# Routing to the best two experts by two rounds of maxima instead of by pairs, and the gate bias added by VectorE instead of TensorE

## The chip, the cores and the metric

The kernel runs on one core of a Trainium2 chip. The metric is the device time of one execution in microseconds (us), the median over several. Three executions of the kernel before took 4944.28, 4973.12 and 4980.82 us; the profiled one, which is another, took 4966.12 us.

## The reference, cut to what matters

The program is a decoder of four layers over 16 sequences (batches) of 100 tokens with 128 features. Every layer has a self attention, a cross attention over a context of 1444 rows, and a feed forward; each adds its result to `x`. The feed forwards of layers 0, 1 and 3 are mixtures of experts with 8, 16 and 8 experts, of which each token uses its best two. For layer 3:

```python
logits = xf @ wg.T + bg
vals, idx = jax.lax.top_k(logits, TOP_K)          # TOP_K = 2
masked = jnp.full_like(logits, -jnp.inf)
masked = masked.at[rows, idx].set(vals)
weights = jax.nn.softmax(masked, axis=-1)
for e in range(NUM_EXPERTS):
    g = xf @ Wgate[e].T
    u = xf @ Wup[e].T
    h = g * jax.nn.sigmoid(g) * u
    out = out + h @ Wdown[e].T * weights[:, e:e + 1]
```

Layer 0 is of the same kind. In layer 1 there is no gate bias in the logits: the experts are picked by the logits plus a bias of their own (`expert_bias`), while the weights are the sigmoids of the logits without it, divided by their sum. When two logits are equal, `top_k` takes the one with the lower index first, and both versions of the kernel keep that.

## The kernel before, in words

One program runs through the stages of the reference in order. Each engine has its own instruction stream, written out by hand, and the order between engines is kept by semaphores alone; there is no planner. `x`, its normalised copy `xn`, and most working tiles lie in SBUF with 128 features on the partitions and the 1600 tokens along the columns. A large tile, `arena`, is shared by the stages. All small weights of a stage are packed in one tile (`w_const` for constants, `w_ff0`, `w_ff1`, `w_ff3` for the gates of the feed forwards; the profile cuts the number off), and each is loaded at the start of the program.

A routed feed forward (the function `feed_forward` of each engine's stream, with `route` for VectorE) runs like this.

1. After the layer normalisation TensorE computes the gate logits, one product for each of the 16 batches, with the tokens of the batch as the stationary operand: a 100 x E block of PSUM bank 0 for each batch (L3516). Where the stage has a gate bias (the first and the third), a product of a row of ones and the bias goes ahead of each of them into the same block (L3515). The last one raises `logits_ready`.
2. VectorE routes (L2436 to L2506). It copies the logits to SBUF (L2442), and in the stages with 8 experts subtracts each token's maximum (L2452, L2455). It then raises `weights_asked`, on which ScalarE computes the exponentials (L1782). Meanwhile VectorE compares every logit of a token with every other one, in tiles of 16 batches x E x E columns: equal to it and of lower index (L2463, L2466), greater than it (L2469), the sum of both (L2472), and a reduction to the rank (L2475). Experts of a rank under 2 are kept (L2478). Then it waits for the exponentials, masks them with that, sums, takes the reciprocal and multiplies (L2490 to L2503).
3. `weights_ready` releases TensorE, which transposes the weights batch by batch (L3521). ScalarE copies them to SBUF (L1787). SP stores them to DRAM (L952), waits for that, and only then loads the first expert's weights (L925) and the rows of its gate weights, spread over the partitions (L935).
4. POOL splits `xn` into a rounded part and a rest at the start of the stage in the stages with 8 experts (L1265, tiles `x_hi` and `x_lo`), later also each expert's weights and the gated tokens. TensorE, ScalarE and VectorE then work through the experts, 128 hidden features and 400 tokens at a time.

On VectorE each instruction of the route raises a semaphore at its end, on which the stream waits before the next one.

Long stages lie in between: the multi-head cross attention of layer 0 from 100 to 1480 us, and the narrow cross attention of layer 2, with 8 features a head, from about 2580 to 3460 us.

Of the kernel before, what the change touches and what calls it, by code (L numbers as in the profile page):

```python
# [23 lines left out]
ALU = mybir.AluOpType  # L24
# [257 lines left out]
def feed_parts(n, p):  # L282

    def wide(w):
        return w.transpose(1, 0, 2).reshape(w.shape[1], -1)

    if n == 0:
        return (chunks_of(wide(p["L0_ffn_w1"]), wide(p["L0_ffn_w3"]), p["L0_ffn_w2"].reshape(-1, 128)),
                dict(gate=p["L0_ffn_gate_w"], gate_b=p["L0_ffn_gate_b"][None]))
    if n == 1:  # L290
        up = [np.concatenate([wide(p[f"L1_ffn_w{k}"].transpose(0, 2, 1)), p[f"L1_ffn_sw{k}"].T], 1) for k in (1, 3)]
        down = np.concatenate([p["L1_ffn_w2"].transpose(0, 2, 1).reshape(-1, 128), p["L1_ffn_sw2"].T], 0)
        bias = [np.concatenate([p[f"L1_ffn_b{k}"].reshape(-1), p[f"L1_ffn_sb{k}"]]) for k in (1, 3)]
        return (chunks_of(up[0], up[1], down, *bias),
                dict(gate=p["L1_ffn_gate_w"].T, expert_b=np.tile(p["L1_ffn_expert_bias"], (128, 1)),
                     b2=p["L1_ffn_b2"], sb2=p["L1_ffn_sb2"][None]))
    if n == 2:
        return (chunks_of(p["L2_ffn_w1"][0], None, p["L2_ffn_w2"][0], p["L2_ffn_b1"][0]),
                dict(b2=p["L2_ffn_b2"][0][None], ln_g=column(p["L2_ffn_gamma"]), ln_b=column(p["L2_ffn_beta"])))
    if n == "g":  # L300
        return (chunks_of(p["L3_xattn_W1"], None, p["L3_xattn_W2"], p["L3_xattn_b1"]), dict(b2=p["L3_xattn_b2"][None]))
    return (chunks_of(wide(p["L3_ffn_Wgate"].transpose(0, 2, 1)), wide(p["L3_ffn_Wup"].transpose(0, 2, 1)),
                      p["L3_ffn_Wdown"].transpose(0, 2, 1).reshape(-1, 128)),
            dict(gate=p["L3_ffn_wg"].T, gate_b=p["L3_ffn_bg"][None]))


def film_parts(p):
# [70 lines left out]
def constants():  # L378

    i = np.arange(128)  # L380
    ident = np.eye(128, dtype=np.float32)
    mean = np.full((128, 128), 1 / 128, np.float32)
    ones = np.ones((128, 128), np.float32)
    row96 = np.zeros((C + 1, C + 1), np.float32)
    row96[C] = 1
    own_head = np.zeros((C + HEADS, HEADS), np.float32)
    for h in range(HEADS):
        own_head[C + h, h] = -1
    head_rows = (i[:, None] // 8 == i[None, :] // 8).astype(np.float32)

    def head_rows_of(n):

        at = np.arange(4 * n)
        return (i[:, None] == (at // n * 32 + at % n)[None, :]).astype(np.float32)

    return dict(ident=ident, mean=mean, ones=ones, row96=row96,
                head_cols=(i[:, None] // 8 % 4 == np.arange(4)[None, :]).astype(np.float32),
                rows8=head_rows_of(9), rows16=head_rows_of(17),
                own_head=own_head, head_rows=head_rows,
                zeros=np.zeros((HEADS, 128), np.float32),  # L400
                ones_row=np.ones((1, GT), np.float32),
                before=np.tile((np.arange(16)[None, :] < np.arange(16)[:, None]).astype(np.float32).reshape(1, -1), (128, 1)))


def build(nc, dram, where, out):
# [1413 lines left out]
    def _(dve):  # L1819
# [615 lines left out]
        def route(n):  # L2435

            cfg = FEED[FF[n]]
            E = cfg["E"]
            dve.wait_ge(s.logits_ready, 1)
            dve.sem_inc(s.logits_ready, -1)  # L2440
            lg, bi, rk, wt = (t[:, :, 0:E] for t in (logits, biased, rank, weight))
            nc.vector.tensor_copy(lg, ps[0:S, 0, 0:B * E].rearrange("p (b e) -> p b e", e=E)).then_inc(s.dve_done, 1)  # L2442
            dve.wait_ge(s.dve_done, 1)
            dve.sem_inc(s.dve_done, -1)
            by = lg
            if cfg.get("sigmoid"):
                nc.vector.tensor_tensor(bi, lg, W(FF[n], "expert_b")[0:S, :].unsqueeze(1).to_broadcast([S, B, E]), ALU.add).then_inc(s.dve_done, 1)
                dve.wait_ge(s.dve_done, 1)
                dve.sem_inc(s.dve_done, -1)
                by = bi  # L2450
            else:
                nc.vector.tensor_reduce(best[:, :], lg, AX.X, ALU.max).then_inc(s.dve_done, 1)  # L2452
                dve.wait_ge(s.dve_done, 1)
                dve.sem_inc(s.dve_done, -1)
                nc.vector.tensor_tensor(lg, lg, best[:, :].unsqueeze(2).to_broadcast([S, B, E]), ALU.subtract).then_inc(s.dve_done, 1)  # L2455
                dve.wait_ge(s.dve_done, 1)
                dve.sem_inc(s.dve_done, -1)
            dve.sem_inc(s.weights_asked, 1)
            p1 = pairs[:, 0:B * E * E].rearrange("p (b e f) -> p b e f", e=E, f=E)
            p2 = pairs2[:, 0:B * E * E].rearrange("p (b e f) -> p b e f", e=E, f=E)  # L2460
            mine, other = by.unsqueeze(3).to_broadcast([S, B, E, E]), by.unsqueeze(2).to_broadcast([S, B, E, E])
            before = W("const", "before")[0:S, :].rearrange("p (e f) -> p e f", f=16)[:, 0:E, 0:E]
            nc.vector.tensor_tensor(p1, other, mine, ALU.is_equal).then_inc(s.dve_done, 1)  # L2463
            dve.wait_ge(s.dve_done, 1)
            dve.sem_inc(s.dve_done, -1)
            nc.vector.tensor_tensor(p1, p1, before.unsqueeze(1).to_broadcast([S, B, E, E]), ALU.mult).then_inc(s.dve_done, 1)  # L2466
            dve.wait_ge(s.dve_done, 1)
            dve.sem_inc(s.dve_done, -1)
            nc.vector.tensor_tensor(p2, other, mine, ALU.is_gt).then_inc(s.dve_done, 1)  # L2469
            dve.wait_ge(s.dve_done, 1)  # L2470
            dve.sem_inc(s.dve_done, -1)
            nc.vector.tensor_tensor(p1, p1, p2, ALU.add).then_inc(s.dve_done, 1)  # L2472
            dve.wait_ge(s.dve_done, 1)
            dve.sem_inc(s.dve_done, -1)
            nc.vector.tensor_reduce(rk, p1, AX.X, ALU.add).then_inc(s.dve_done, 1)  # L2475
            dve.wait_ge(s.dve_done, 1)
            dve.sem_inc(s.dve_done, -1)
            nc.vector.tensor_scalar(rk, rk, 2.0, None, ALU.is_lt).then_inc(s.dve_done, 1)  # L2478
            dve.wait_ge(s.dve_done, 1)
            dve.sem_inc(s.dve_done, -1)  # L2480
            dve.wait_ge(s.weights_exp, 1)
            dve.sem_inc(s.weights_exp, -1)
            if cfg.get("sigmoid"):
                nc.vector.tensor_scalar(wt, wt, 1.0, None, ALU.add).then_inc(s.dve_done, 1)
                dve.wait_ge(s.dve_done, 1)
                dve.sem_inc(s.dve_done, -1)
                nc.vector.reciprocal(wt, wt).then_inc(s.dve_done, 1)
                dve.wait_ge(s.dve_done, 1)
                dve.sem_inc(s.dve_done, -1)
            nc.vector.tensor_tensor(wt, wt, rk, ALU.mult).then_inc(s.dve_done, 1)  # L2490
            dve.wait_ge(s.dve_done, 1)
            dve.sem_inc(s.dve_done, -1)
            nc.vector.tensor_reduce(best[:, :], wt, AX.X, ALU.add).then_inc(s.dve_done, 1)
            dve.wait_ge(s.dve_done, 1)
            dve.sem_inc(s.dve_done, -1)
            if cfg.get("sigmoid"):
                nc.vector.tensor_scalar(best[:, :], best[:, :], 1e-10, None, ALU.add).then_inc(s.dve_done, 1)
                dve.wait_ge(s.dve_done, 1)
                dve.sem_inc(s.dve_done, -1)
            nc.vector.reciprocal(best[:, :], best[:, :]).then_inc(s.dve_done, 1)  # L2500
            dve.wait_ge(s.dve_done, 1)
            dve.sem_inc(s.dve_done, -1)
            nc.vector.tensor_tensor(wt, wt, best[:, :].unsqueeze(2).to_broadcast([S, B, E]), ALU.mult).then_inc(s.dve_done, 1)  # L2503
            dve.wait_ge(s.dve_done, 1)
            dve.sem_inc(s.dve_done, -1)
            dve.sem_inc(s.weights_ready, 1)  # L2506
# [255 lines left out]
    def _(pe):  # L2762
# [740 lines left out]
        def feed_forward(n):  # L3503
# [6 lines left out]
            if cfg["gate"]:  # L3510
                E = cfg["E"]
                for b in range(B):
                    to = bank(0, E, S, b * E)
                    if "gate_b" in where[w]:
                        mm(to, W("const", "ones")[0:1, 0:S], W(w, "gate_b"), start=True, stop=False)  # L3515
                    ins = mm(to, xn[:, b, :], W(w, "gate"), start="gate_b" not in where[w], stop=True)  # L3516
                ins.then_inc(s.logits_ready, 1)
                pe.wait_ge(s.weights_ready, 1)
                pe.sem_inc(s.weights_ready, -1)
# [108 lines left out]
```

## Time and profile before

| | |
|---|---|
| median of three executions | 4973.12 us (4944.28 to 4980.82) |
| profiled execution | 4966.12 us, its span 4964.2 us |
| mean granted TensorE clock | 0.879 of full speed |
| TensorE (PE) busy | 86%, 27918 matmul records |
| VectorE (DVE) busy | 56%, 4307 instructions |
| ScalarE (ACT), POOL busy | 40%, 33% |
| routed stages in the span | about 1506, 2112 and 4685 us |

The span runs from the first to the last instruction of the profiled execution. A timeline row gives the start in the span, the duration, the engine, the source line, the operation, the tile written and the tiles read, shapes as partitions x columns, and in brackets how long the engine had been idle and what released it. A float32 product leaves two records in the profile. The granted clock is given as a share of full speed: 1.00 is 2.4 GHz and 0.50 is 1.2 GHz.

### The profile page before, as it was taken

How to read it: one execution, taken by the hardware profiler on the slowest of the kernel's cores; microseconds unless marked ns; L12 is line 12 of the kernel's file. 1: busy time of each engine (PE TensorE's matmuls, PEld its weight loads, DVE VectorE, ACT ScalarE, POOL GpSimd, SP SyncE). 2: the span in 40 equal slices, each digit the busy share in tenths (PEclk: the TensorE clock that was granted, in tenths of full speed). 3: DMA queues.
4: the chain of work that ended last, by engine and by line, in shares of the span. 5: the costliest groups of instructions: out<-in, count | busy, mean ns of one | idle time of the engine just before them, and what ended most of it. 6: DMA issues, size and time to landing. Idle time of an engine off the chain costs nothing. (4 is left out here: it accounts for less than half of the span.)

```text
span 4964.2 us, 88758 instructions
## 1 busy us (share of the span) xinstructions
PE 4246.6 (86%) x27918; PEld 2986.8 (60%) x27918; DVE 2781.1 (56%) x4307; ACT 1978.0 (40%) x3118; POOL 1662.4 (33%) x1320
## 2 busy tenths in 40 slices
PE   8899999999998988967879999999695666756799
PEld 4578888888876855834445555555353444444477
DVE  4344454454433443545634666665536999987433
ACT  2255555555542223213423455454233444440222
POOL 2255666666643323102421113230032343320042
PEclk8799999999997989979955899998796888878699
DMA  2000000000001210420011223221001011100021
GB/s 88 1 10 19 10 19 10 19 19 10 19 1 40 61 25 19 109 64 17 2 33 34 58 56 67 55 58 40 0 2 36 23 32 28 28 16 0 1 64 48
DMA packets 124783, 154.03 MB, mean 31 GB/s; under 512 B 86928, under 2 KB 110240, under 8 KB 124224
## 3 DMA queue, kind: packets, MB, share of 16 engines
q1 hardware_dynamic: 124352, 148.54, 12.0%
q8 instruction: 239, 3.92, 0.3%
q14 instruction: 192, 1.57, 0.1%
HBM read 110.25 MB, written 2.66 MB: 23 GB/s over the span
## 5 line engine op out<-in xcount | busy, mean ns | idle before, releaser
L1046 POOL TENSOR_TENSOR pexp_lo<-arena,pexp_hi 128x800 fp32r<-128x800 f32 x384 | 636.2, 1657 | 435.8 <-POOLq L1045 435.8
L2381 DVE TENSOR_REDUCE arena<-ps 100x1 f32<-100x482 f32 (+1 forms) x768 | 490.7, 657 | 287.9 <-DVEq L2368 278.8
L2261 DVE TENSOR_REDUCE arena<-ps 128x1 f32<-128x482 f32 (+3 forms) x624 | 392.9, 656 | 361.4 <-DVEq L2239 351.4
L1529 ACT ACTIVATE arena<-ps 128x800 f32<-128x800 f32 x384 | 322.1, 839 | 495.9 <-ACTq L1527 493.7
L3300 PE MATMUL ps<-kst,qs 96*100 96x482 f32 (+1 forms) x768 | 389.1, 509 | 41.1 <-PEq L3254 37.7
L1629 ACT ACTIVATE arena<-ps 128x800 f32<-128x800 f32 x384 | 315.4, 836 | 260.7 <-ACTq L1628 260.4
L992 POOL TENSOR_TENSOR max_diag<-w_const,arena 100x800 fp32r<-100x800 f32 x160 | 246.7, 1542 | 448.3 <-POOLq L990 448.3
L2573 DVE MATCH_REPLACE8 arena<-arena 128x1444 f32<-128x1444 f32 x208 | 340.8, 1645 | 0.0
L1530 ACT ACTIVATE pexp_hi<-ps 128x800 fp32r<-128x800 f32 x384 | 319.6, 832 | 0.0
L2675 DVE TENSOR_TENSOR arena<-ps,arena 128x400 f32<-128x400 f32 x256 | 147.0, 574 | 282.1 <-DVEq L2674 282.1
L2034 DVE TENSOR_REDUCE arena<-ps 100x8 f32<-100x800 f32 x160 | 158.2, 991 | 259.2 <-DVEq L2031 259.2
L3565 PE MATMUL ps<-arena,chunk 128*128 128x400 f32 x648 | 279.7, 514 | 15.4 <-PEq L3564 14.6
L3184 PE MATMUL ps<-pexp_hi,ctxk_hi 128*97 128x400 f32 (+1 forms) x768 | 276.8, 360 | 2.4 <-PEq L3179 2.0
L3165 PE MATMUL ps<-qa_hi,ctxT_hi 113*128 113x400 f32 (+1 forms) x768 | 273.8, 356 | 1.4 <-PEq L3159 1.4
L3426 PE MATMUL ps<-ctxT,arena 97*128 97x482 f32 (+7 forms) x408 | 190.6, 686 | 94.4 <-PEq L3423 94.4
L3166 PE MATMUL ps<-qa_lo,ctxT_hi 113*128 113x400 f32 (+1 forms) x768 | 265.6, 346 | 0.0
L3167 PE MATMUL ps<-qa_hi,ctxT_lo 113*128 113x400 f32 (+1 forms) x768 | 265.3, 345 | 0.0
L1449 ACT ACTIVATE arena<-ps 100x800 f32<-100x800 f32 x160 | 133.9, 837 | 328.2 <-ACTq L1448 328.1
L3185 PE MATMUL ps<-pexp_hi,ctxk_lo 128*97 128x400 f32 (+1 forms) x768 | 264.6, 344 | 0.0
L3137 PE MATMUL ps<-ctxT_hi,qa_hi 113*128 113x482 f32 (+3 forms) x624 | 256.1, 411 | 6.6 <-PEq L3110 5.5
L1801 ACT ACTIVATE arena<-ps 128x400 f32<-128x400 f32 x256 | 128.9, 503 | 332.9 <-ACTq L1798 332.9
L1239 POOL TENSOR_TENSOR xn<-arena,mid 128x482 fp32r<-128x482 f32 (+1 forms) x48 | 58.0, 1209 | 585.4 <-POOLq L1238 585.4
(396 smaller groups left out, 9535.9 us busy)
## 6 DMA issues: line engine op xcount, KB each, us to landing
ctxT<-in_ctxT SPq DMA_DIRECT2D x56, 541.5 KB
kst<-mid SPq DMA_DIRECT2D x128, 180.5 KB, 3.1
ctxk<-in_ctx SPq DMA_DIRECT2D x40, 528.0 KB
chunk<-in_ff_chunks SPq DMA_DIRECT2D x77, 193.0 KB, 2.4
arena<-gate_dram SPq DMA_DIRECT2D x64, 200.0 KB, 3.9
kst<-xn SPq DMA_DIRECT2D x64, 180.5 KB, 2.9
arena<-gate_dram SPq DMA_DIRECT2D x64, 100.0 KB, 2.6
arena<-in_ctxT SPq DMA_DIRECT2D x8, 541.5 KB
```

The source lines that it names most:

```text
L1046: own(nc.gpsimd.tensor_tensor(pexp_lo[p % 3][:, :, :], pexp[p % 3], pexp_hi[p % 3][:, :, :], ALU.subtract))
L1529: nc.scalar.activation(pexp[p % 3], of, ACT.Exp, scale=scale).then_inc(s.pexp_ready, 1)
L1530: own(nc.scalar.activation(pexp_hi[p % 3][:, :, :], of, ACT.Exp, scale=scale))
L1629: nc.scalar.activation(pexp2[p % 3], ps[:, 2 * (p % 2):2 * (p % 2) + 2, 0:GT], ACT.Exp, scale=scale).then_inc(s.pexp_ready, 1)
L2261: peak = nc.vector.tensor_reduce(mparts[0:at.stop - at.start, m, c:c + 1], bank(k, z - a, at.stop - at.start), AX.X, ALU.max)
L2381: peak = nc.vector.tensor_reduce(mparts2[:, h, c:c + 1], bank(k, z - a, S), AX.X, ALU.max)
L2573: nc.vector.match_replace(left[k], tops[:, k, at], scores_sb[i] if r == 0 else left[k], TAKEN).then_inc(done[i], 1)
L3165: mm(o, ctxT_hi[par][:, keys], qa_hi[par][:, q], start=True, stop=False)
L3166: mm(o, ctxT_hi[par][:, keys], qa_lo[par][:, q], start=False, stop=False)
L3184: mm(o, ctxk_hi[par][0:r, t, :], hi, start=t == 0, stop=False, skip_group_check=True)
L3300: ins = mm(bank(k, z - a, S), qs[par][0:C, g, S * (h % 4):S * (h % 4) + S], kst[0:C, g, a:z], start=True, stop=True)
L3565: ins = mm(bank(4 + g), chunk[c][:, 256:384], h_all[k], start=False, stop=last)
```

## The change

The 16 x 16 table of "lower index" among the constants gives way to a row of 16 descending numbers (16 down to 1), `order`. The gate bias is stored once on each of the 128 partitions instead of in one row; TensorE's bias products go, and VectorE adds the bias while it brings the logits from PSUM. The best expert is found by a maximum over the logits, an equality with it, and a second maximum over `order` where they are equal, so that of equal ones the lowest index is taken. That one is then lowered by 3e38, and the second best is found in the same way. Every instruction works on 16 batches x E columns. In the stage with 16 experts the request for the exponentials now comes before the addition of the expert bias.

```diff
-                dict(gate=p["L0_ffn_gate_w"], gate_b=p["L0_ffn_gate_b"][None]))
+                dict(gate=p["L0_ffn_gate_w"], gate_b=np.tile(p["L0_ffn_gate_b"], (128, 1))))
...
-                before=np.tile((np.arange(16)[None, :] < np.arange(16)[:, None]).astype(np.float32).reshape(1, -1), (128, 1)))
+                order=np.tile(np.arange(16, 0, -1, dtype=np.float32), (128, 1)))
...
-            nc.vector.tensor_copy(lg, ps[0:S, 0, 0:B * E].rearrange("p (b e) -> p b e", e=E)).then_inc(s.dve_done, 1)
...
+            first, rest = (t[:, 0:B * E].rearrange("p (b e) -> p b e", e=E) for t in (pairs, pairs2))
+            order = W("const", "order")[0:S, 0:E].unsqueeze(1).to_broadcast([S, B, E])
+            per_token = best[:, :].unsqueeze(2).to_broadcast([S, B, E])
+
+            def own(ins):
+                ins.then_inc(s.dve_done, 1)
                 dve.wait_ge(s.dve_done, 1)
                 dve.sem_inc(s.dve_done, -1)
+
+            raw = ps[0:S, 0, 0:B * E].rearrange("p (b e) -> p b e", e=E)
+            by = lg
+            if "gate_b" in where[FF[n]]:
+                own(nc.vector.tensor_tensor(lg, raw, W(FF[n], "gate_b")[0:S, :].unsqueeze(1).to_broadcast([S, B, E]), ALU.add))
+            else:
+                own(nc.vector.tensor_copy(lg, raw))
+            if cfg.get("sigmoid"):
+                dve.sem_inc(s.weights_asked, 1)
+                own(nc.vector.tensor_tensor(bi, lg, W(FF[n], "expert_b")[0:S, :].unsqueeze(1).to_broadcast([S, B, E]), ALU.add))
                 by = bi
...
-            nc.vector.tensor_tensor(p1, other, mine, ALU.is_equal).then_inc(s.dve_done, 1)
-            nc.vector.tensor_tensor(p1, p1, before.unsqueeze(1).to_broadcast([S, B, E, E]), ALU.mult).then_inc(s.dve_done, 1)
-            nc.vector.tensor_tensor(p2, other, mine, ALU.is_gt).then_inc(s.dve_done, 1)
-            nc.vector.tensor_tensor(p1, p1, p2, ALU.add).then_inc(s.dve_done, 1)
-            nc.vector.tensor_reduce(rk, p1, AX.X, ALU.add).then_inc(s.dve_done, 1)
-            nc.vector.tensor_scalar(rk, rk, 2.0, None, ALU.is_lt).then_inc(s.dve_done, 1)
+            own(nc.vector.tensor_reduce(best[:, :], by, AX.X, ALU.max))
+            own(nc.vector.tensor_tensor(by, by, per_token, ALU.subtract))
+            if not cfg.get("sigmoid"):
+                dve.sem_inc(s.weights_asked, 1)
+            own(nc.vector.scalar_tensor_tensor(rk, by, 0.0, order, ALU.is_equal, ALU.mult))
+            own(nc.vector.tensor_reduce(best[:, :], rk, AX.X, ALU.max))
+            own(nc.vector.tensor_tensor(first, rk, per_token, ALU.is_equal))
+            own(nc.vector.scalar_tensor_tensor(rest, first, TAKEN, by, ALU.mult, ALU.add))
+            own(nc.vector.tensor_reduce(best[:, :], rest, AX.X, ALU.max))
+            own(nc.vector.tensor_tensor(rk, rest, per_token, ALU.is_equal))
+            own(nc.vector.tensor_tensor(rk, rk, order, ALU.mult))
+            own(nc.vector.tensor_reduce(best[:, :], rk, AX.X, ALU.max))
+            own(nc.vector.tensor_tensor(rk, rk, per_token, ALU.is_equal))
+            own(nc.vector.tensor_tensor(rk, rk, first, ALU.add))
...
-                    if "gate_b" in where[w]:
-                        mm(to, W("const", "ones")[0:1, 0:S], W(w, "gate_b"), start=True, stop=False)
-                    ins = mm(to, xn[:, b, :], W(w, "gate"), start="gate_b" not in where[w], stop=True)
+                    ins = mm(to, xn[:, b, :], W(w, "gate"), start=True, stop=True)
```

The gate bias of the third routed stage (`L3_ffn_bg`) is stored in the same way as that of the first. `TAKEN` is -3e38.

## Rows read from the trace of the kernel before

**Rows 1.** The page's engine totals: busy us, share of the span, instructions.
```profile
PE 4246.6 (86%) x27918; PEld 2986.8 (60%) x27918; DVE 2781.1 (56%) x4307; ACT 1978.0 (40%) x3118; POOL 1662.4 (33%) x1320
```

**Rows 2.** Windows: length, busy PE, PEld, DVE, ACT, POOL, then PE clock, DMA share, GB/s.
```profile
1506.60:1520.60 14.00, 13.80 (x64) 12.99 (x64) 0.00 (x0) 0.00 (x0) 5.07 (x2) 0.50 0.00 1
1520.60:1531.20 10.60, 0.00 (x0) 0.00 (x1) 8.34 (x13) 1.59 (x2) 0.00 (x0) 0.50 0.00 0
...
1541.60:1553.00 11.40, 9.34 (x23) 6.78 (x23) 3.87 (x6) 2.79 (x4) 7.94 (x11) 0.50 0.26 88
...
4685.40:4687.00 1.60, 1.51 (x12) 1.43 (x12) 0.00 (x0) 0.00 (x0) 1.33 (x1) 1.00 0.00 0
4687.10:4698.40 11.30, 11.23 (x53) 10.55 (x52) 0.00 (x0) 0.00 (x0) 3.64 (x2) 0.50 0.01 1
```

**Rows 3.** Windows of the gate products alone, second stage: PE, PEld, clock, DMA.
```profile
2112.00:2113.40 1.40, 1.32 (x16) 1.35 (x16) 1.00 0.05 12
2113.50:2116.40 2.90, 2.88 (x18) 2.77 (x17) 0.50 0.00 0
```

**Rows 4.** Timeline of the first stage's route, from the last gate product.
```profile
1519.98 0.50 PE L3516 MATMUL ps<-w_ff,xn 128*100 128x8 f32 x2
1520.63 0.29 DVE L2442 COPY arena<-ps 100x128 f32<-100x128 f32 x1 [14.39 <-DVEq L2440]
1521.07 0.28 DVE L2452 TENSOR_REDUCE arena<-arena 100x16 f32<-100x128 f32 x1
1521.50 0.29 DVE L2455 TENSOR_TENSOR arena<-arena 100x128 f32<-100x128 f32 x1
1522.03 1.23 DVE L2463 TENSOR_TENSOR arena<-arena 100x1024 f32<-100x1024 f32 x1 [0.24 <-DVEq L2457]
...
1523.34 0.31 ACT L1782 ACTIVATE arena<-arena 100x128 f32<-100x128 f32 x1
...
1528.88 0.23 DVE L2478 TENSOR_SCALAR arena<-arena 100x128 f32<-100x128 f32 x1
1529.37 0.29 DVE L2490 TENSOR_TENSOR arena<-arena 100x128 f32<-100x128 f32 x1 [0.26 <-DVEq L2482]
```

**Rows 5.** Timeline of the second stage's route, 16 experts.
```profile
2117.10 0.43 DVE L2447 TENSOR_TENSOR arena<-arena,w_ff 100x256 f32<-100x256 f32 x1
2117.76 4.43 DVE L2463 TENSOR_TENSOR arena<-arena 100x4096 f32<-100x4096 f32 x1 [0.24 <-DVEq L2449]
...
2141.18 0.29 DVE L2484 TENSOR_SCALAR arena<-arena 100x256 f32<-100x256 f32 x1 [0.26 <-DVEq L2482]
```

**Rows 6.** Groups of VectorE instructions by shape: busy us, mean ns, idle before.
```profile
L2050 DVE SCALAR_TENSOR_TENSOR arena<-squares,col,arena 100x256 f32<-100x256 f32 x16 | 16.8, 1051 | 3.8 <-DVEq L1979 3.8
L2047 DVE TENSOR_TENSOR arena<-ps,arena 100x128 f32<-100x128 f32 x48 | 14.0, 291 | 7.2 <-DVEq L1979 0.2
...
L2640 DVE SCALAR_TENSOR_TENSOR squares<-deviation,squares 128x400 f32<-128x400 f32 x4 | 2.3, 575 | 0.6 <-DVEq L2638 0.3
...
L2609 DVE SCALAR_TENSOR_TENSOR squares<-xn,kernel_l,squares 128x128 f32<-128x128 f32 x2 | 0.6, 346 | 0.0
```

**Rows 7.** Timeline of the first stage: POOL's split, SP's first weights, gated tokens.
```profile
1508.55 3.55 POOL L1265 TENSOR_TENSOR x_lo<-xn,x_hi 128x1600 fp32r<-128x1600 f32 x1 [0.18 <-POOLq L1268]
...
1537.54 0.38 SPq L925 DMA_DIRECT2D chunk<-in_ff_chunks  x1
...
1543.84 0.87 DVE L2665 TENSOR_TENSOR squares<-xn,arena 128x400 f32<-128x400 f32 x1 [0.44 <-DVEq L2664]
```

**Rows 8.** Windows of the narrow cross attention, columns as in rows 2.
```profile
2640.00:2740.00 100.00, 99.63 (x707) 61.53 (x706) 47.54 (x79) 34.21 (x46) 10.05 (x19) 0.50 0.19 42
2920.00:3020.00 100.00, 92.97 (x1071) 57.44 (x1073) 69.78 (x121) 51.46 (x71) 20.85 (x38) 1.00 0.27 61
```

**Rows 9.** DMA issues (KB, us to landing), and VectorE's first instruction in the timeline.
```profile
w_const<-in_const SPq DMA_DIRECT2D x1, 758.5 KB, 6.0
...
9.17 0.06 DVE L2730 MEMSET root_there<- 1x2 f32 x1 [9.17 <-DMA w_sa<-in_sa]
```

More of the change, by code:

```diff
@@ L303, in feed_parts @@
                       p["L3_ffn_Wdown"].transpose(0, 2, 1).reshape(-1, 128)),
-            dict(gate=p["L3_ffn_wg"].T, gate_b=p["L3_ffn_bg"][None]))
+            dict(gate=p["L3_ffn_wg"].T, gate_b=np.tile(p["L3_ffn_bg"], (128, 1))))
 def film_parts(p):
@@ L2441, in route @@
             lg, bi, rk, wt = (t[:, :, 0:E] for t in (logits, biased, rank, weight))
-            nc.vector.tensor_copy(lg, ps[0:S, 0, 0:B * E].rearrange("p (b e) -> p b e", e=E)).then_inc(s.dve_done, 1)
[L2443 to L2447, printed above, removed]
+            first, rest = (t[:, 0:B * E].rearrange("p (b e) -> p b e", e=E) for t in (pairs, pairs2))
@@ L2448, in route @@
+            order = W("const", "order")[0:S, 0:E].unsqueeze(1).to_broadcast([S, B, E])
+            per_token = best[:, :].unsqueeze(2).to_broadcast([S, B, E])
+            def own(ins):
+                ins.then_inc(s.dve_done, 1)
                 dve.wait_ge(s.dve_done, 1)
                 dve.sem_inc(s.dve_done, -1)
-                by = bi
[L2451 to L2462, printed above, removed]
-            nc.vector.tensor_tensor(p1, other, mine, ALU.is_equal).then_inc(s.dve_done, 1)
@@ L2464, in route @@
-            dve.wait_ge(s.dve_done, 1)
-            dve.sem_inc(s.dve_done, -1)
-            nc.vector.tensor_tensor(p1, p1, before.unsqueeze(1).to_broadcast([S, B, E, E]), ALU.mult).then_inc(s.dve_done, 1)
-            dve.wait_ge(s.dve_done, 1)
-            dve.sem_inc(s.dve_done, -1)
-            nc.vector.tensor_tensor(p2, other, mine, ALU.is_gt).then_inc(s.dve_done, 1)
-            dve.wait_ge(s.dve_done, 1)
-            dve.sem_inc(s.dve_done, -1)
-            nc.vector.tensor_tensor(p1, p1, p2, ALU.add).then_inc(s.dve_done, 1)
@@ L2473, in route @@
-            dve.wait_ge(s.dve_done, 1)
-            dve.sem_inc(s.dve_done, -1)
-            nc.vector.tensor_reduce(rk, p1, AX.X, ALU.add).then_inc(s.dve_done, 1)
-            dve.wait_ge(s.dve_done, 1)
-            dve.sem_inc(s.dve_done, -1)
-            nc.vector.tensor_scalar(rk, rk, 2.0, None, ALU.is_lt).then_inc(s.dve_done, 1)
-            dve.wait_ge(s.dve_done, 1)
-            dve.sem_inc(s.dve_done, -1)
+            raw = ps[0:S, 0, 0:B * E].rearrange("p (b e) -> p b e", e=E)
+            by = lg
```

## The prediction

> **What bounds the kernel now.** I read the engine totals first, then the timeline round the three routed feed forwards, then windows with the granted clock. TensorE is busy for 86% of the span [rows 1], but that is an average: in the three places that the change touches it either runs tiny products or stands still. In the first expert stage its gate products take 13.80 us at clock 0.50, and then it does nothing for 10.6 us while VectorE routes (8.34 busy) [rows 2]. The chain of waits of the whole program ended at once and showed nothing, so I followed the semaphores by hand: the last gate product releases the route's first copy, the route's last multiplication releases the transposes, their copies release the store of the gates, and SP issues the first expert weight load, at 1537.54, only after that store [rows 7]. TensorE, VectorE, ScalarE, POOL and SP all stand behind the route. So in these stretches a microsecond off the gate products or off VectorE is a microsecond off the end; there is no cover to look for.
>
> **Bias products, first and third stage.** 16 gate products alternate with 16 bias products. Each product leaves two records, and 64 records take 13.80 us: 0.43 us a product at clock 0.50 [rows 2]. What will 16 uniform products cost? The second stage has no gate bias and shows it: 16 records in 1.35 us at clock 1.00, so 0.17 us a product, and about 16.5 records in 2.88 us at 0.50, so 0.35 us [rows 3]. I take those, since they are the same products with the same alternation gone; 0.43 is the bound above.
> - First stage, clock 0.50 throughout [rows 2]: 16 x 0.35 = 5.6 instead of 13.8, **gain 8.2** (6.9 at 0.43; 11.1 if all of it ran at 0.17).
> - Third stage: the clock is 1.00 for 1.6 us, then 0.50 [rows 2]; together 1.51 + 11.23, some 12.8 us of products. 1.6 / 0.17 = 9.4 products fit before the fall, the other 6.6 cost 0.35: 3.9 us, **gain 8.9**. With alternating prices (12 records in 1.51 us, so 0.25, then 0.43) it is 6 x 0.25 + 10 x 0.43 = 5.8 and a gain of 7.0; all at 0.17, 10.1.
>
> **Route with 8 experts, twice.** Removed are five instructions over 1024 columns and one over 128, from 1522.03 to the start of the weighting at 1529.37: 7.34 us [rows 4]. Ten over 128 columns take their place: three reductions, two with a scalar and two tensors, five with two tensors. A reduction starts its successor 0.43 us after its own start, a two-tensor instruction 0.44 us [rows 4]. The old last instruction took 0.23 us and the next started 0.49 us after it, so the wait for the exponentials adds 0.11. The form with a scalar has no row at this size; with a constant scalar it costs 575 ns at 400 columns, and 346 ns with a scalar per partition at 128 [rows 6], and the slope between the 128 and 1024 columns of two tensors (0.29 and 1.23 [rows 4]) gives 0.57 at 400 as well. I take 0.29, as the scalars here are constants. 10 x 0.437 + 0.11 = 4.5, **gain 2.9 each**. If the slow row decides (1051 ns at 256 columns, where 575 at 400 says that something else slows it [rows 6]), two instructions lose 0.3 each and the gain is 2.3.
>
> **Route with 16 experts.** From 2117.76 to 2141.18 are 23.42 us, most of it five instructions over 4096 columns, 4.43 us the first [rows 5]. The maximum and the subtraction are new here, so 12 instructions come in. The addition over 256 columns took 0.43, and with the 0.145 us from an end to the successor's start [rows 4] one costs 0.57 [rows 5]: 12 x 0.57 + 0.11 = 6.95, **gain 16.5** (15.3 with the slow row).
>
> **What I cost at nothing, and its cover.** The bias rides on the copy out of PSUM: an addition from PSUM over 128 columns costs 291 ns [rows 6], the copy 0.29 [rows 4]. The exponentials end 1.6 us after the request (1522.03 to 1523.65) [rows 4], the new ten instructions last 4.4: 2.8 us of cover are left, and if it were gone at most the 1.6 would show. In the second stage the request only moves ahead of the addition. POOL's split of the tokens ends at 1512.10 in the first stage [rows 7], the shortened products at 1506.6 + 5.6 = 1512.2. In the third it outlives them by about 1.5 us, and a VectorE instruction beside POOL's took 0.87 instead of 0.57 at 400 columns [rows 7]: three small ones, 0.1 each, **loss 0.3**. No step moves past another queue: the loads stay in place, and the gate bias fills rows that the packed file already had. The constants shrink by 240 of 1517 columns, 120 KB of 758.5 KB in 6.0 us [rows 9]: between 0 and 0.95 us at the start; I take 0, as VectorE's first instruction waits for a later load, until 9.17 [rows 9].
>
> **Sum.** 8.2 + 8.9 + 2.9 + 2.9 + 16.5 - 0.3 = 39.1 us. The profiled execution took 4966.1 us (its span and 1.9 us round it), 7.0 under the median of the runs, 4973.1, and equal to the mean of all four times; 4966.1 - 39.1 = **4927 us**, -0.8%. The bounds together: gains of 33 to 45 us, 4921 to 4933. The runs of before spread by 36.5 us, so a median of the changed kernel may fall some 17 us to either side.
>
> **Rivals.**
> - **The clock comes out better.** After the pause the first stage's expert products still run for 11.4 us at 0.50, with TensorE busy for 9.34 [rows 2]. A pause that is 2.9 us shorter may end that sooner, for 5 us a stage at most (half of the 9.34). More hangs on a later stretch: with TensorE 99.6% busy the clock stayed at 0.50 for 100 us from 2640, which issued 707 products, where the same stage issues 1071 at clock 1.00 [rows 8]. Those 100 us are worth 34. If the shift of all that follows ends this stretch early, the time is about 4893. For it: the stretch looks like chance, since TensorE was as busy as later. Against: nothing in the change reaches it but the shift. Chance 0.18.
> - **The clock comes out worse: slower than before.** The same mechanism, placed in the narrow cross attention after 2580: the shifted work keeps the half rate longer. Each us there costs 0.34, so the gain is eaten from 39.1 / 0.34 = 115 us more; a stretch that covers 160 us more gives 4927 + 54 = 4981. Products removed ahead of it are work that the clock may have counted, but they sit over 1000 us earlier, and the clock was 0.50 right through them [rows 2]. Chance 0.10, and for a loss of over 1% (280 us more) 0.03.
> - **The number of instructions decides, not their size.** Then 4 more instructions at 8 experts and 7 at 16 cost 0.15 to 0.16 fixed and 0.145 between, 0.3 each: 15 x 0.3 = 4.5 us lost, only the 17.1 less 0.3 of the products won, 4954. Against it: 1024 columns cost 1.23 and 128 cost 0.29 [rows 4], 4096 cost 4.43 [rows 5], so the size does decide. Chance 0.04. The Trainium skill says as much ("VectorE: DVE Perf Modes", Rules for kernel authors: for chained operations keep their count low), and its section on the errata there advises operands of 512 elements or more; by that this change goes the wrong way. The trace agrees that there is a fixed cost and not with what would follow here: the fixed 0.3 us is less than the 0.93 us that 896 columns fewer save [rows 4].
> - **The products don't shorten the chain**, because something else releases the route (POOL, or the logits' bank). Then only 2.9 + 2.9 + 16.5 are left, 4944. VectorE's copy starts 0.15 us after the last product's end [rows 4], which speaks against it. Chance 0.04.
>
> **How the numbers follow.** The forecast has 0.64. A change within 1%, about what a measurement of this kernel can tell from none, is 4923.4 to 5022.9 us against the median. The forecast at 4927 lies 4 us inside that border with 17 of spread, so about 0.38 of it falls below: 0.24. The better clock adds 0.16. Faster by over 1%: 0.40; slower by over 1%: 0.03, from the worse clock; the rest, 0.57, within. The range: 4895 leaves out about 0.1, the better part of the better clock; 4960 leaves out about 0.1, most of the worse clock, and holds the cases at 4944 and 4954.
>
> **What would show it.** In the changed trace: 32 records of gate products instead of 64 in the first stage, in 5 to 7 us; from the route's first instruction to the transposes 7.6 to 7.8 us in the first stage, and 16 to 17 us less than before in the second; 17 and 22 VectorE instructions; the exponentials done before they are asked for; everything behind unchanged relative to the transposes, the rise of the clock included. It is wrong if a small instruction costs more than 0.35 us at 128 columns, if the uniform products keep 0.43, or if the stages behind last longer by the clock. The stages before 1500 should not change at all.

## The result: some 22 us faster, 4933.85 us where 4927 was predicted

Twenty executions of the changed kernel took 4933.85 us in the median (4887.18 to 5030.07), twenty of the kernel before beside them 4955.57 (4930.24 to 5016.96); the ratio is 0.9935, with a 95% interval of 0.9907 to 0.9963. Two further timings of the same changed kernel gave 0.9964 (0.9919 to 1.0010) and 0.9987 (0.9943 to 1.0031). All executions together have a mean of 4942.2 us (44, standard error 4.9) against 4964.3 (114, 2.6): 22.1 us less, with a standard error of 5.5. Ratios leave out executions over 1.5% above a kernel's fastest, which cuts a continuous spread at an odd place here, so I use means of all executions, with their standard errors, beside them.

So it is faster, by about 0.45%, which is within 1%. The local gains came out as predicted up to the transposes (38.7 us for 39.1), and with the stages behind them a little larger (42.6); about half of that did not reach the mean. Both need showing.

**Engines.** The page's totals: 64 matmul records fewer, 14 VectorE instructions more than in [rows 1].
```profile
PE 4321.6 (86%) x27854; PEld 3021.4 (60%) x27854; DVE 2763.5 (55%) x4321; ACT 1979.0 (40%) x3118; POOL 1662.0 (33%) x1320
```

**Gate products and pauses.** Windows of the first and of the third stage, columns as in [rows 2].
```profile
1504.00:1509.60 5.60, 5.47 (x32) 5.41 (x32) 0.00 (x0) 0.00 (x0) 5.08 (x2) 0.50 0.01 3
1509.60:1517.40 7.80, 0.00 (x0) 0.03 (x1) 4.89 (x17) 1.59 (x2) 0.00 (x0) 0.50 0.00 0
...
4733.80:4735.40 1.60, 1.51 (x18) 1.55 (x18) 0.00 (x0) 0.00 (x0) 1.34 (x1) 1.00 0.00 0
4735.40:4738.00 2.60, 2.55 (x17) 2.46 (x16) 0.00 (x0) 0.00 (x0) 2.42 (x2) 0.51 0.00 0
```
The first stage's 32 records take 5.47 us at clock 0.50 where 64 took 13.80, and VectorE does 17 instructions in 4.89 us where it did 13 in 8.34 [rows 2].

**The first route**, a timeline from the products to the first expert's load (to set beside [rows 4, 7]).
```profile
1504.04 5.47 PE L3508 MATMUL ps<-w_ff,xn 128*100 128x8 f32 x32 [1.17 <-PEq L3503]
1505.90 3.56 POOL L1265 TENSOR_TENSOR x_lo<-xn,x_hi 128x1600 fp32r<-128x1600 f32 x1 [0.18 <-POOLq L1268]
1509.66 0.29 DVE L2454 TENSOR_TENSOR arena<-ps,w_ff 100x128 f32<-100x128 f32 x1 [6.07 <-DVEq L2440]
1510.10 0.29 DVE L2461 TENSOR_REDUCE arena<-arena 100x16 f32<-100x128 f32 x1
1510.53 0.29 DVE L2462 TENSOR_TENSOR arena<-arena 100x128 f32<-100x128 f32 x1
1511.07 0.29 DVE L2465 SCALAR_TENSOR_TENSOR arena<-arena,w_const 100x128 f32<-100x128 f32 x1 [0.25 <-DVEq L2449]
...
1512.37 0.31 ACT L1782 ACTIVATE arena<-arena 100x128 f32<-100x128 f32 x1
...
1514.99 0.29 DVE L2474 TENSOR_TENSOR arena<-arena 100x128 f32<-100x128 f32 x1
1515.54 0.29 DVE L2484 TENSOR_TENSOR arena<-arena 100x128 f32<-100x128 f32 x1 [0.26 <-DVEq L2476]
...
1517.40 2.83 PE L3513 MATMUL ps<-w_const,arena 100*8 100x100 f32 x16 [7.89 <-PEq L3511]
...
1523.72 0.38 SPq L925 DMA_DIRECT2D chunk<-in_ff_chunks  x1
```
Each of the ten picking instructions takes 0.29 us, the form with a constant scalar (L2465) too. The exponentials are done at 1512.68, 2.9 us before they are used. From the first gate product to the first transpose it is 13.36 us (24.55 before), and SP's load still follows the transposes by 6.3 us (1517.40 to 1523.72; before 1531.23 to 1537.54).

**The second route**, with 16 experts (to set beside [rows 5]).
```profile
2100.27 0.42 DVE L2456 COPY arena<-ps 100x256 f32<-100x256 f32 x1 [4.99 <-DVEq L2440]
...
2102.64 0.42 DVE L2465 SCALAR_TENSOR_TENSOR arena<-arena,w_const 100x256 f32<-100x256 f32 x1
...
2108.81 0.29 DVE L2478 TENSOR_SCALAR arena<-arena 100x256 f32<-100x256 f32 x1 [0.61 <-DVEq L2476]
...
2113.73 2.83 PE L3513 MATMUL ps<-w_const,arena 100*16 100x100 f32 x16 [13.61 <-PEq L3511]
```
TensorE stands still for 13.61 us ahead of the transposes, where it stood for 29.72.

**Where it was lost.** The profiled execution of the changed kernel took 5001.17 us, 35 more than that of before, although each route is shorter. The stretch from the end of the second routed stage to the third's first gate product accounts for it. The two kernels' code does not differ there; the windows say this of the changed kernel
```profile
2221.15:4733.89 2512.74, 2012.98 (x15141) 1238.64 (x15141) 1662.62 (x2376) 961.28 (x1572) 591.67 (x428) 0.79 0.12 28
```
and this of the kernel before:
```profile
2255.23:4685.49 2430.26, 1908.32 (x15140) 1182.34 (x15141) 1658.25 (x2376) 960.34 (x1572) 591.50 (x428) 0.83 0.12 29
```
The work is the same, 15,140 matmul records; the granted clock is 0.79 against 0.83, and the stretch is 82.5 us longer. One execution of each is no verdict on the change, so the experiments ask whether this is chance.

### The profile page after: what moved, and what is told of

Read it like the earlier page. It is cut to its first block and busy times, and to the rows that moved or that the text cites. A ratio compares the mean times of both kernels' runs of the same rounds, so it can differ in the third digit from the quotient of the medians.

```text
span 4999.0 us, 88658 instructions
## 1 busy us (share of the span) xinstructions
PE 4321.6 (86%) x27854; PEld 3021.4 (60%) x27854; DVE 2763.5 (55%) x4321; ACT 1979.0 (40%) x3118; POOL 1662.0 (33%) x1320
## 3 DMA queue, kind: packets, MB, share of 16 engines
HBM read 110.12 MB, written 2.66 MB: 23 GB/s over the span
## 5 line engine op out<-in xcount | busy, mean ns | idle before, releaser
L3294 PE MATMUL ps<-kst,qs 96*100 96x482 f32 (+1 forms) x768 | 425.3, 555 | 37.1 <-PEq L3248 33.5
L3557 PE MATMUL ps<-arena,chunk 128*128 128x400 f32 x648 | 277.5, 510 | 16.7 <-PEq L3556 16.1
L3420 PE MATMUL ps<-ctxT,arena 97*128 97x482 f32 (+7 forms) x408 | 213.4, 761 | 88.2 <-PEq L3417 88.2
L3332 PE MATMUL ps<-arena 128*32 128x100 f32 x6144 | 264.5, 295 | 0.6 <-PEq L3351 0.4
```

The costliest lines, as they stand in the source:

```text
L3294: ins = mm(bank(k, z - a, S), qs[par][0:C, g, S * (h % 4):S * (h % 4) + S], kst[0:C, g, a:z], start=True, stop=True)
L3557: ins = mm(bank(4 + g), chunk[c][:, 256:384], h_all[k], start=False, stop=last)
```

## The experiments

Unless something else is said, each is the changed kernel with one edit, timed in 12 executions. "Routed stages" below is the sum, in one trace, of the three stretches from the first gate product to the last addition to `x`. It is 692.8 and 694.3 us in two traces of the kernel before, and 650.4, 650.4 and 652.0 in three of the changed kernel.

**Each half of the change alone.** Only the bias moved, the ranking by pairs kept:
```diff
-            own(nc.vector.tensor_reduce(best[:, :], by, AX.X, ALU.max))
...
+            nc.vector.tensor_tensor(p1, other, mine, ALU.is_equal).then_inc(s.dve_done, 1)
...
```


> Only the gate bias moves to VectorE; the routing by pairs stays. My theory (every us off the gate products is off the end): gate products of the first stage 5.5 us instead of 13.8, of the third 4 to 5.6 instead of 12.8, the routes unchanged at 10.6 and 29.5 us from first instruction to the transposes; 17 us less in all, near 4939 us where the kernel before stands at 4956. Rival, that something else releases the route: 4956. Rival, that the clock of later stages follows the change: the stretches shrink by 17 us, the total by another amount, and the stages after 2500 us show it.

Only the picking by rounds, the gate bias kept as a product:
```diff
-                own(nc.vector.tensor_tensor(lg, raw, W(FF[n], "gate_b")[0:S, :].unsqueeze(1).to_broadcast([S, B, E]), ALU.add))
+            own(nc.vector.tensor_copy(lg, raw))
...
+                    if "gate_b" in where[w]:
+                        mm(to, W("const", "ones")[0:1, 0:S], W(w, "gate_b"), start=True, stop=False)
```


> Only the routing by rounds; the gate bias stays a product on TensorE. My theory: gate products 13.8 and 12.8 us as before, routes 7.7 us (first, third stage) and 13 to 13.5 us (second); 22 us less in all, near 4934 us. Rival, the number of instructions decides: 4.5 us more than before, 4960. Rival, the clock of later stages follows the change: the total moves by another amount than the stretches.

Measured: 4957.17 us and 4967.95, ratios 1.0011 (0.9971 to 1.0050) and 0.9931 (0.9892 to 0.9969). Both totals miss their forecasts of 4939 and 4934. What the traces show below would give ratios of 0.9963 and 0.9953: the second interval holds that, the first leaves it out. Executions of one kernel differ by more than these effects, so the totals do not decide here. Groups of matmuls of the first one (records | busy us, mean ns | idle before):
```profile
L3518 PE MATMUL ps<-w_ff,xn 128*100 128x8 f32 x64 | 9.6, 292 | 2.3 <-PEq L3513 2.3
L3523 PE MATMUL ps<-w_const,arena 100*8 100x100 f32 x32 | 5.7, 370 | 21.6 <-PEq L3521 21.6
```
and of the second:
```profile
L3512 PE MATMUL ps<-w_const,arena 100*8 100x100 f32 x32 | 5.6, 370 | 15.8 <-PEq L3510 15.8
...
L3512 PE MATMUL ps<-w_const,arena 100*16 100x100 f32 x16 | 2.8, 371 | 13.6 <-PEq L3510 13.6
```
With the bias alone the products of both stages take 9.6 us and the pauses stay at 21.6; with the rounds alone the pauses are 15.8 and 13.6, as in the whole change. The halves add up: the routed stages are 675.2 and 670.4 us, 18.4 and 23.2 under before, together 41.6 against the 42.6 of both at once.

**The ten picking instructions, five times over** (the repeats compute the same again):
```diff
+            for again in range(5):
```


> The changed kernel with its ten picking instructions run five times in each routed stage (the repeats compute the same again), so 40 small instructions more in each. My theory (0.44 us each at 128 columns, 0.57 at 256, all on the path): 17.5 + 22.8 + 17.5 = 58 us more than the changed kernel, near 4992 us; the route takes 25 us in the first stage and 36 in the second. If only the fixed part counted (0.3 each): 36 us more. If the pause were covered by something: no more. If a longer pause of TensorE also delayed the rise of its clock: over 58, by up to 5 a stage.

Measured: 4980.90 us, ratio 1.0015 (0.9979 to 1.0051).
```profile
L3514 PE MATMUL ps<-w_const,arena 100*8 100x100 f32 x32 | 5.7, 371 | 50.9 <-PEq L3512 50.9
...
L3514 PE MATMUL ps<-w_const,arena 100*16 100x100 f32 x16 | 2.8, 371 | 36.1 <-PEq L3512 36.1
```
The pauses grew from 16.0 and 13.6 us to 50.9 and 36.1, so by 57.4: all of it is on the path, with 0.436 us an instruction at 8 experts (34.9 / 80) and 0.56 at 16 (22.5 / 40). But the mean over the executions is 4977.9 us, only 35.7 above the changed kernel (standard error 8.8). Locally the theory holds; the total falls short of it.

**Four picking instructions instead of ten.** The order by index among equal logits is left out.
```diff
-            own(nc.vector.scalar_tensor_tensor(rk, by, 0.0, order, ALU.is_equal, ALU.mult))
...
+            own(nc.vector.tensor_scalar(first, by, 0.0, TAKEN, ALU.is_equal, ALU.mult))
+            own(nc.vector.tensor_tensor(rest, first, by, ALU.add))
...
+            own(nc.vector.tensor_tensor(rk, by, per_token, ALU.is_ge))
```


> The changed kernel with four VectorE instructions in place of the ten that pick the experts (equality with the maximum times -3e38, addition, second maximum, and 'greater or equal' against it). The order by index among equal logits is left out. Theory (each small instruction costs its duration plus 0.145 us on the path): six instructions fewer, 0.44 us each at 8 experts (two stages) and 0.57 at 16 experts, so the pause of TensorE ahead of the transposes falls from 7.9 to about 5.3 us in the first and third stage and from 13.6 to about 10.2 in the second: 8.7 us less than the changed kernel, a ratio to the kernel before of about 0.992. But at 8 experts only five instructions of 0.44 stand between the request for the exponentials and the weighting, 2.2 us against 1.6 for the exponentials, so their cover holds. Rival (the exponentials or the transposes set the end): the pauses stay above 7 us. The total alone will not show it, since the clock moves single executions by tens of us.

Measured: 4934.69 us, ratio 0.9908 (0.9861 to 0.9954).
```profile
L3507 PE MATMUL ps<-w_const,arena 100*8 100x100 f32 x32 | 5.6, 368 | 11.0 <-PEq L3505 11.0
...
L3507 PE MATMUL ps<-w_const,arena 100*16 100x100 f32 x16 | 2.8, 368 | 9.7 <-PEq L3505 9.7
```
The pauses fall by 8.9 us where 8.7 were expected: VectorE's instructions still set the pause, not the exponentials.

**The products that open the accumulators, moved into the pause**, with what cannot move left behind the transposes:
```diff
+                opened()
                 pe.wait_ge(s.weights_ready, 1)
...
+            if n == 1:
+                for g in range(NG):
+                    mm(bank(4 + g), W(w, "b2"), gateT[0:16, g * GT:g * GT + GT], start=False, stop=False)
```


> The changed kernel with TensorE's eight (second stage: four of eight) accumulator-opening products moved ahead of its wait for the weights, into the pause of the route. My theory (the clock is not moved by this, the opening is hidden behind the loads in the first and third stage): nothing there, 4 to 5 us less in the second stage, where they run until 10 us after the store of the gates; near 4929 us. Rival, the clock counts work in the pause: the rise to full speed comes earlier after the transposes, up to 5 us less in each stage beside that, near 4917.

and once more, with more executions:

> The changed kernel with the accumulator-opening products moved into the pause, once more and with more executions. Theory (the moved products are off the path only in the second stage, where TensorE went straight from the transposes to them): from the second stage's first transpose to its end 102 us instead of 107.4, the first and third stage unchanged within 1.5 us, so about 5 us less than the changed kernel at the same granted clock. Rival (its 15 us by the first ratios, 0.9857 against 0.9935, were the clock's doing): no difference at the same clock; then the second stage's end must have moved back.

Measured: 4918.48 us in 6 executions, ratio 0.9857 (0.9808 to 0.9907), and 4941.75 in 12, ratio 0.9973 (0.9934 to 1.0011). The first of these looked like the best kernel of all; but its six executions ran from 4873 to 5046 us, and the repeat shows that the ratio was chance. Behind the transposes, the second stage of the repeat is a chain of 8 records of opening products where the changed kernel has 16:
```profile
2119.89 2.83 PE L3519 MATMUL ps<-w_const,arena 100*16 100x100 f32 x16 [7.97 <-PEq L3517]
2123.73 5.67 PE L3526 MATMUL ps<-arena,w_ff 16*128 16x400 f32 x8 [1.01 <-PEq L3523]
```
That stage is 102.1 us from the transposes to its end (107.4 in the changed kernel); the other two are within 1.5 us, since TensorE then waits for the first expert's weights instead, 7.70 us in the first stage where the changed kernel shows 0.99:
```profile
1534.16 0.67 PE L3552 MATMUL ps<-x_hi,w_hi 128*128 128x400 f32 x1 [7.70 <-PEq L3535]
```
The routed stages are 647.0 and 645.2 us, 4.8 under the changed kernel; the mean of all 18 executions is 4945.6 (standard error 10.3), not to be told from it. At the same granted clock, by a straight line of time against clock through both kernels' executions, they are 2.0 us under it (1.4), where about 5 were expected.

**The same with the first expert's weights loaded ahead of the store of the gates:**
```diff
+                weights(0, 0)
...
+                    ahead = cfg["gate"] and c == 0
+                    if not ahead:
```


> The changed kernel with the accumulator-opening products moved into the pause (as in the run before of that kind) and the first expert's weights loaded ahead of the store of the gates. Theory (behind the transposes the path runs over the store of the gates and then the first weight load): TensorE's first expert product no longer waits 7.6 us for weights, and the first and third stage get up to 5 us shorter each; the second, which got 5 to 7 us shorter by the moved products alone, keeps that. About 15 us less than the changed kernel, a ratio of about 0.985 with the run of the moved products at 0.9857. Rival (the gate rows, which need the store, set the first product's successors as well): the first products start early but the stage's end stays within 1 us, and nothing is gained over the moved products alone.

Measured: 4932.66 us, ratio 0.9992 (0.9947 to 1.0037), mean 4937.1.
```profile
1534.22 0.67 PE L3554 MATMUL ps<-x_hi,w_hi 128*128 128x400 f32 x1 [1.17 <-PEq L3537]
...
1536.54 2.64 SPq L935 DMA_DIRECT2D arena<-gate_dram  x4
...
1542.62 0.67 PE L3554 MATMUL ps<-xg_hi,w_hi 128*128 128x400 f32 x1 [7.06 <-PEq L3541]
```
The rival was right: the first product starts 1.17 us after the transposes, and the second then waits 7.06 us for the tokens gated with the stored rows. The routed stages are 642.6 us, 3.5 under the run before it.

**Both kernels again, unaltered.**

> The changed kernel once more, not altered. Theory (what the changed stretches gain is fixed, what the clock does in the narrow cross attention is chance): from the first gate product to the first transpose again 13.4 and 18.0 us in the first and second stage, to within 0.3, while the narrow cross attention lasts anything between 815 and 931 us, by its granted clock. Rival (the shift of the work made the narrow stage slower, 931 us in the changed kernel's first profile against 854): it lasts over 910 us again. Ratio to the kernel before 0.9935, within 0.004.

> The kernel before once more, not altered. Theory: from the first gate product to the first transpose 24.6 and 34.0 us in the first and second stage as in its first profile, and the narrow cross attention anything between 815 and 931 us. Rival (its length belongs to the kernel): 854 us again, within 5.

> The changed kernel for the third time, beside the one with the moved products. Theory: mean over the executions 29 us below the kernel before, within 10, and at equal granted clock 25 us below it, within 3.

Measured: the changed kernel 4940.35 and 4951.82 us, the kernel before 4926.54 in its one execution. The third timing missed its forecast: the mean, 4950.7 us, is 13.6 below the kernel before (10.2 below the executions beside it), where 29, within 10, was expected; at the same granted clock it is 21.7 below those beside it (standard error 1.6), where 25, within 3, was. From the first gate product to the first transpose the changed kernel shows 13.36 and 19.09 us, then 12.19 and 19.09, the kernel before 24.55 and 35.20; where a figure differs by about 1.1 from its first trace, a part of the gate products ran at another clock. The same unchanged stretch as above, in the second trace of the changed kernel
```profile
2234.11:4675.37 2441.26, 1924.44 (x15141) 1185.06 (x15141) 1660.52 (x2376) 960.54 (x1572) 592.42 (x428) 0.82 0.12 29
```
and in the second trace of the kernel before:
```profile
2259.50:4645.80 2386.30, 1858.14 (x15141) 1149.26 (x15141) 1655.21 (x2376) 960.25 (x1572) 592.22 (x428) 0.85 0.13 30
```
So the same kernel takes 2512.7 or 2441.3 us for it, the other 2430.3 or 2386.3, by its clock. The narrow cross attention inside lasted 931, 870 and 850 us in three traces of the changed kernel, 854 and 815 in two of the kernel before. The rival that its length belongs to the kernel is out; a tendency on top of the chance is not.

The clock varies ahead of every edited instruction too. The first routed stage's gate products start at 1506.7 and 1507.8 us in the two traces of the kernel before, at 1504.0, 1517.1 and 1517.5 in those of the changed one. A window in the third of these traces, columns as in [rows 2], and the same window in the first trace of the kernel before:
```profile
1415.00:1435.00 20.00, 18.58 (x45) 12.66 (x46) 4.87 (x9) 5.24 (x8) 5.32 (x3) 0.54 0.01 1
1415.00:1435.00 20.00, 20.00 (x94) 15.21 (x94) 8.72 (x15) 9.90 (x13) 9.73 (x7) 1.00 0.01 2
```
This late part of the multi-head cross attention runs at the lower clock in the one trace and at the full clock in the other.

**The ten instructions 11 and 25 times over,** to see that tendency, if there is one, against a shift far above the chance (6 executions each):

> The changed kernel with the ten picking instructions done 11 times over. By the run with five times, each repeat costs 14.35 us on the three paths, so the three routed stages get 143.5 us longer than in the changed kernel, 794 us in all against 651. Theory (the rest of the program runs on unchanged): mean time 4942 + 143 = 5085 us, and the mean granted clock falls by about 0.011, to 0.867. Rival (the clock gives back what TensorE stands still: over the runs so far each us taken out of the routed stages was worth 0.57 us, 0.10 standard error): 4942 + 0.57 x 143 = 5024 us, with the mean granted clock still near 0.878.

> The changed kernel with the ten picking instructions done 25 times over: 24 x 14.35 = 344 us more on the three paths, 995 us for the three routed stages. Theory (the rest runs on unchanged): 5286 us, mean granted clock 0.854. Rival (the clock gives back): 4942 + 0.57 x 344 = 5138 us, clock near 0.878. If it gives back only for pauses of a few tens of us, this run comes out near 5286 less some constant 20 to 60 us.

Measured: 5047.03 us, ratio 1.0171 (1.0126 to 1.0216), and 5256.81, ratio 1.0593 (1.0539 to 1.0648), at mean granted clocks of 0.878 and 0.862. The means are 5044.6 and 5252.9. Neither of the first two forecasts holds for both (5085 and 5286 if the rest ran on unchanged, 5024 and 5138 if the clock gave back 0.43 of each us); the third does, that a bounded amount comes back, here 40 and 33 us. With "the rest" as the mean of all executions less the routed stages of the traces (the error is that of the mean; only the traced executions tell the routed stages):

| kernel | routed stages | mean of executions | the rest |
|---|---|---|---|
| before | 693.6 | 4964.3 | 4270.7 (2.6) |
| changed | 650.9 | 4942.2 | 4291.3 (4.9) |
| bias alone | 675.2 | 4965.2 | 4290.0 (7.9) |
| rounds alone | 670.4 | 4964.9 | 4294.5 (12.0) |
| four instructions | 642.0 | 4928.5 | 4286.5 (9.3) |
| opened in the pause | 646.1 | 4945.6 | 4299.5 (10.3) |
| and weights ahead | 642.6 | 4937.1 | 4294.5 (7.0) |
| ten, 5 times | 708.8 | 4977.9 | 4269.1 (7.3) |
| ten, 11 times | 795.1 | 5044.6 | 4249.5 (2.7) |
| ten, 25 times | 997.4 | 5252.9 | 4255.5 (7.8) |

All six kernels with shorter routes than before have a longer rest; the three with longer routes have the same or a shorter one, by 21 us at most. The rest holds no edited instruction.

The row of the kernel before puts executions of several chips together. Those beside the bias alone, the rounds alone and the five times, on one chip, have a mean of 4975.2 us, those beside the others between 4959.8 and 4961.5. Measured against the executions beside it, the changed kernel's rest is 24.5 us longer (standard error 5.8), that of the bias alone and of the rounds alone only 8 and 13 (10 and 13), and that of the ten instructions 5, 11 and 25 times is 13, 17 and 11 us shorter (9, 7 and 10). So the longer rest of the whole change stands; of the two halves it is not shown.

## Why the prediction was right, point by point

- **The bias products: right.** Forecast 5.6 us for the first stage, measured 5.47; third stage 3.9 against 4.07. Gains of 8.3 and 8.8 where 8.2 and 8.9 stood. The second stage's products were the right rows to price them by.
- **The routes with 8 experts: right.** Pauses of 7.89 and 8.09 us instead of 10.75 twice: 2.86 and 2.66 against 2.9 each. The scalar form costs 0.29, so the slow row at 256 columns was not a row to price by.
- **The route with 16 experts: right, 0.4 short.** The pause is 16.1 us shorter, forecast 16.5; a wait of 0.61 instead of 0.26 us ahead of L2478 is most of that. There are 21 VectorE instructions, not 22, a miscount of mine in the signs and in a rival, not in the sum.
- **POOL's cover: right, and smaller.** In the third stage one instruction took 0.49 us instead of 0.29 beside POOL, a loss of 0.2 for the 0.3 forecast.
- **The sum: 39.1 us forecast, 38.7 measured** from the first gate products to the transposes (11.19 + 16.02 + 11.44). Behind the transposes 1.7 and 2.1 us more came in the second and third stage, which the forecast had at nothing (109.1 to 107.4, 251.0 to 248.9; the third trace lacks the last of these, 250.4).
- **The number of instructions does not decide.** With 4 and 6 more instructions (not 7) the pauses shrank by 2.9 and 16.1 us. What the rule of the Trainium skill ("VectorE: DVE Perf Modes", Rules for kernel authors) is about shows only once the sizes are equal: ten instructions down to four gave 8.9 us.
- **"Nothing in the change reaches it but the shift": the step that failed.** The clock's rivals were placed in the stretch in which the traces differ most, behind 2580, but treated as chance alone, with the mean kept at the forecast. Stages that last longer by the clock were the prediction's own last sign of being wrong. The rest was 20.6 us longer in the mean (standard error 5.5), with repeats of the picking it was up to 21.2 shorter than before. So about half of the 42.6 us was given back. The worse clock in its full size (4981) did not come, and the better one (4893) did not either.
- **"The stages before 1500 should not change at all": not shown.** The stretch ahead of the first routed stage was 10 us longer in two of the three traces of the changed kernel, by its clock. Of the smaller constants' load the first trace shows VectorE's first instruction at 8.84 us instead of 9.17, within the 0.95 allowed.
- **Why the number was close all the same.** 4966.1 - 39.1 = 4927 becomes, with the measured terms, 4964.3 - 42.6 + 20.6 = 4942.3 in the mean, and the median of the first twenty executions, 4933.85, lies below that by the chance that single executions show. The closeness is partly luck; the sum of the local terms is not.

How the rest comes to depend on the routed stages stays open. What is shown: it holds no edit, its length goes with the granted clock, and longer routed stages go with a shorter rest until about 100 us more than before. Whether it is the stillness of TensorE, the products that are gone, or the position in time of what follows, was not separated; and as the traces differ ahead of the first routed stage too, it is not shown that all of the longer rest lies behind the change.

## What to carry to other kernels

Add up a change on the critical path from the rows around it, and test that sum on the same stretch of the new trace, not on the total. Where TensorE works at a clock that varies from execution to execution, the total needs many executions, and a local gain may not reach it whole, here only by half. A kernel that looks best in six executions is to be run again before anything is built on it.

## What the runs showed of the hardware that I had not expected

- Over the 44 executions of the changed kernel the time follows the mean granted clock almost alone: correlation -0.99, 37 to 38 us for each 0.01 of clock. Nearly all of the spread, 4887 to 5030 us, goes with the clock.
- The same 8180 matmul records of the narrow cross attention took 815.2 us at a mean granted clock of 0.94 and 930.6 at 0.77, with TensorE busy for 93% and 95% of it:
```profile
2601.90:3417.10 815.20, 754.08 (x8180) 461.89 (x8179) 549.60 (x940) 396.52 (x545) 173.31 (x237) 0.94 0.26 57
```
  is the second trace of the kernel before, and of the changed kernel's first:
```profile
2564.80:3495.40 930.60, 882.25 (x8180) 543.96 (x8179) 554.22 (x940) 397.76 (x545) 172.90 (x237) 0.77 0.23 50
```
  The Trainium skill ("TensorE: Matmul & The Clock Gate", Part 1) says that the throttled clock is the state at rest and that activity releases it. By that sentence alone a stretch as busy as this one would keep the full clock. The rows differ: a mean of 0.77 is the lower level for 46% of the stretch, a mean of 0.94 for 12%, and in the table longer routed stages, with more stillness of TensorE in the repeats, go with a shorter rest.
- Products with one row and with 128 rows as the stationary operand, in turn, cost more than uniform ones: 64 records took 13.80 us, 0.216 each, and 32 with 128 rows throughout 5.47, 0.171 each, both at clock 0.50. Whether the turns or the one row cost it was not separated.
